# A second attention in phases of twelve tiles instead of eight, with its side steps placed ahead of each phase's last four tiles

## The chip, the cores and the metric

The kernel runs on one core of a Trainium2 chip. The metric is the device time of one execution in microseconds (us), lower is better. Before the change it is 3915.79 us, the median of three runs (3913.46 to 3922.16).

## What is computed

The program is one block of a hybrid model on x of 4 x 1024 tokens with 256 features, all in fp32: a causal attention, a mixture of experts, a second attention, and the mixture again, each added to its input. Only the second attention is changed. Cut to what matters:

```python
Xn = layernorm(X)                                  # x itself is a layernorm of the stage's input
P = einsum('btd,ed->bte', Xn, W_in) + b_in         # Q, K, V and a gate G, 16 heads of 16
sq = |Q|^2 + |K|^2 - 2 Q K^T                       # 1024 x 1024 per head, no causal mask
W = (1e-4 + sqrt(max(sq, 0))) ** -2
W = W / (1e-4 + sum(W))
out = X + einsum('btd,ed->bte', G * (W V), W_out) + b_out
```

## The kernel before

The stage is `attention_b`. A **unit** is one batch with one group of four heads (16 units); a **period** j is a unit with one half of its queries (512), 32 in all. In a period the keys are worked through in eight **tiles** m of 128 keys. So there are 256 tiles, g = 8 j + m. In the code b, p = divmod(j, 8): batch b, and period p of it. A tile passes through these steps, with `w` as its buffer of 128 x (4 heads x 512) values:

- `dist` on TensorE (L1958): squared distances of keys and queries, in two pairs of heads, each pair into one slot of a PSUM ring of **three slots**.
- `log` on ScalarE (L1869): logarithm of a pair from its slot into `w`; gives the slot back. It needs the table "natural_log" (loaded at L1919), and that the tile of `w` is free, which the values that last used it signal (`s_pv`).
- `bound` on VectorE (L1775): a lower bound for the logarithm.
- sigmoid on ScalarE (L1909), with the table "sigmoid_and_others" (loaded at L1906).
- squaring on VectorE (L1831): `w` times itself, the finished weight; signals `s_wts`.
- `values` on TensorE (L1946): weights times values, summed over a period's eight tiles in `acc`; it waits for `s_wts`.

Since logarithm and sigmoid are in different tables, ScalarE goes in blocks: eight sigmoids of a period, then eight logarithms of the next. VectorE makes eight squarings, then eight bounds.

Around that are **side steps**, in which TensorE takes one slot of the ring each:

- `tokens`: transposes the normalised tokens of a batch (L1971), copied out by ScalarE (L1877); `moments` (L1717) and `normalise` (L1732) on VectorE come before.
- `qkv` (n, x), L1982: projection for unit n, in two halves. VectorE's `take` (L1747 to L1755) reads the slot and gives it back. ScalarE squares Q and K (`squared`, L1893), VectorE sums them up (`lengths`, L1762).
- `stack` (n, i), L1992: transposes Q or K with their lengths; it waits until both `lengths` of the unit are done. VectorE's `operand` (L1769) copies it out and gives the slot back.
- `back` (j), L1999: transposes the finished sums of a period. It waits for `o_rows` (L1780, a copy of `acc` to `oT` on VectorE, which signals `s_oT`). `gates` (L1791 to L1796) on VectorE reads the slot, gives it back, and gates and normalises the result.
- `turn` and `project` (L1971, L2006, L2008), twice a batch: transpose the gated result (copied by ScalarE, `turned`, L1885) and project it, the bias by a matmul of its own. `add` (L1804) on VectorE gives the slot back.

TensorE works through one list, `ORDER`, in order. The other engines have their orders written out as loops; they and TensorE wait for each other by semaphores alone. An engine that waits in its list holds all that stands behind. A side step waits for its slot of the ring to be free, in the list's order of slots, as `dist` does: a slot comes round every third use.

In the order before, a plain period of TensorE is: values of tiles 0 to 2 with side steps between and behind them, the first distances of the next period, then values 3 and 4, and distances and values in turn, and the last four distances at the end:

```python
            if m == TB - 5:
                out += aux + ahead[:1]
            elif m > TB - 4:
                out += ahead[m - TB + 4:m - TB + 5]
            elif m < TB - 5:
                out += aux[:1]
```

`o_rows(j)` stands among the bounds after the period's squarings, and `gates(j)` ahead of the next period's squarings.

Of the kernel before, what the change touches and what calls it, by code (L numbers as in the profile page):

```python
# [22 lines left out]
P = 128  # L23
# [1483 lines left out]
def attention_b(nc, block, c, X, x, W, sem):  # L1507
# [11 lines left out]
    LAST = 2  # L1519
    SPAN = TB * P  # L1520

    def moved(j):

        out = [("back", j - 1, 0)] if 0 < j <= PERIODS else []
        b, p = divmod(j, TB)
        if j % 2 == 0 and j // 2 + 1 < UNITS:
            out += [("qkv", j // 2 + 1, x) for x in range(2)]
        if j % 2 and (j + 1) // 2 < UNITS:
            out += [("stack", (j + 1) // 2, i) for i in range(SIDES)]
        if p == 4 and b + 1 < B:  # L1530
            out += [("tokens", b + 1, x) for x in range(2)]
        if p < 2 and 0 < b < B or j > PERIODS:
            out += [("turn", b - 1, p), ("project", b - 1, p)]
        return out

    def first():

        out = [("tokens", 0, x) for x in range(2)] + [("qkv", 0, x) for x in range(2)]
        out += [("stack", 0, i) for i in range(SIDES)]
        return out + [("dist", 0, m) for m in range(TB)]  # L1540

    def order(j):

        ahead = [("dist", j + 1, m) for m in range(TB)] if j + 1 < PERIODS else []
        aux = moved(j)
        if j >= PERIODS:
            return aux
        if j == PERIODS - 1:
            last = [("values", j, m) for m in range(TB)]
            return aux + [("turn", B - 1, 0)] + last[:5] + [("project", B - 1, 0)] + last[5:]  # L1550
        out = aux[:2]
        aux = aux[2:]
        for m in range(TB):
            if m == TB - 5:
                out += aux + ahead[:1]
                aux = []
            elif m > TB - 4:
                out += ahead[m - TB + 4:m - TB + 5]
            elif m < TB - 5:
                out += aux[:1]  # L1560
                aux = aux[1:]
            out += [("values", j, m)]
        return out + ahead[4:]

    ORDER = [step for j in range(PERIODS + 2) for step in ((first() if j == 0 else []) + order(j))]
# [7 lines left out]
    with ExitStack() as ctx:  # L1573
# [5 lines left out]
        b_out = sb("b_out", [1, D])  # L1579
        row = sb("row", [1, P])  # L1580
# [10 lines left out]
        square = sb("square", [P, 2, TILES, HG, 2, DH])  # L1591
# [6 lines left out]
        w = sb("w", [P, TB, HG, QC])  # L1598
# [23 lines left out]
        s_last = sem("b_last_weights_ready")  # L1622
# [9 lines left out]
        def one(m):  # L1632
            return w[:, m].rearrange("p h n -> p (h n)")
# [18 lines left out]
        @block.sync  # L1652
        def _(sp):
            xv = x[0:B * L, :].rearrange("(t p) d -> p t d", p=P)
            for b in range(B):
                sp.dma_start(X[:, b * TB:(b + 1) * TB, :], xv[:, b * TB:(b + 1) * TB, :]).then_inc(s_x[b], 16)
                if b:
                    continue
                sp.dma_start(win[:], W["W_in"].rearrange("(c p) n -> p c n", p=P)).then_inc(s_w, 16)
                sp.dma_start(wo[:], W["W_out"].rearrange("(c p) n -> p c n", p=P)).then_inc(s_w, 16)  # L1660
                sp.dma_start(b_in[:], W["b_in"].partition_broadcast(P)).then_inc(s_w, 16)
                sp.dma_start(b_out[:], W["b_out"].unsqueeze(0)).then_inc(s_w, 16)

        WLOADS = 4 * 16
        INITS = 6

        @block.gpsimd
        def _(pool):
# [9 lines left out]
            def residual(b):  # L1678

                pool.drain()  # L1680
                pool.tensor_scalar(grow[:], rstd[:], 1.0, None, ALU.add)
                pool.tensor_tensor(drop[:], rstd[:], mv[:, :, 0], ALU.mult)
                pool.drain()
                pool.wait_ge(s_xn, b + 1)
                for t in range(TB):
                    pool.tensor_scalar(tile(b, t), tile(b, t), grow[:, t:t + 1], drop[:, t:t + 1], ALU.mult, ALU.subtract)
                pool.drain().then_inc(s_xadd, 1)
# [7 lines left out]
            pool.memset(row[:], 1.0).then_inc(s_init, 1)  # L1695
# [12 lines left out]
        def _(dve):  # L1708
# [26 lines left out]
            def take(n, x):  # L1735
# [14 lines left out]
                if n > 1:  # L1750
                    dve.wait_ge(s_pv, TB * 2 * (n - 1))
                    dve.wait_ge(s_gate, 2 * (n - 1))
# [19 lines left out]
            def bound(j, m):  # L1772

                R.wait_free(dve, AT["dist", j, m] + PAIRS - 1 + SLOTS, ())
                v.tensor_scalar(one(m), one(m), LOG_MIN, None, ALU.max).then_inc(s_bound, 1)  # L1775
# [45 lines left out]
            for m in range(TB):  # L1821
                bound(0, m)
            for j in range(PERIODS):
                b, p = divmod(j, TB)
                if j:
                    gates(j - 1)
                n = j // 2 + 1
                for m in range(TB):
                    if j < PERIODS - 1 or m < TB - LAST:
                        dve.wait_ge(s_sig, TB * j + m + 1)  # L1830
                        v.tensor_tensor(one(m), one(m), one(m), ALU.mult).then_inc(s_wts, 1)  # L1831
                    if n < UNITS:
                        if j % 2 == 0:
                            if m < 2:
                                take(n, m)
                            if m in (4, 5):
                                lengths(n, m - 4)
                        elif m < SIDES:
                            operand(n, m)
                    if b and p < 2 and m == 6:  # L1840
                        add(b - 1, p)
                    if j == PERIODS - 1 and m == TB - LAST:
                        add(B - 1, 0)
                for m in range(TB if j + 1 < PERIODS else 0):
                    bound(j + 1, m)
                    if m == 3:
                        o_rows(j)
                    if b + 1 < B and m == 3:
                        if p == 1:
                            moments(b + 1)  # L1850
                        if p == 3:
                            normalise(b + 1)
            o_rows(PERIODS - 1)
            gates(PERIODS - 1)
            add(B - 1, 1)
# [3 lines left out]
        def _(act):  # L1859
            s = nc.scalar  # L1860

            def log(j, m):

                at = AT["dist", j, m]
                if j:
                    act.wait_ge(s_pv, TB * (j - 1) + m + 1)
                for pair in range(PAIRS):
                    R.wait_ready(act, at + pair, ())
                    s.activation(w[:, m, 2 * pair:2 * pair + 2, :].rearrange("p h n -> p (h n)"), slot(at + pair), ACT.Ln,  # L1869
                                 scale=SHEP_EPS ** -2).then_inc(R.free[(at + pair) % SLOTS], 1)  # L1870
# [30 lines left out]
            for m in range(TB):  # L1901
                log(0, m)
            for j in range(PERIODS):
                b, p = divmod(j, TB)
                n = j // 2 + 1
                s.preload_act_table_set("sigmoid_and_others")  # L1906
                for m in range(TB):
                    act.wait_ge(s_bound, TB * j + m + 1)
                    s.activation(one(m), one(m), ACT.Sigmoid, scale=-0.5).then_inc(s_sig, 1)  # L1909
                    if j % 2 == 0 and n < UNITS and m in (3, 5):  # L1910
                        squared(n, (m - 3) // 2)
                    if p == 4 and b + 1 < B and m in (2, 4):
                        tokens(b + 1, m // 2 - 1)
                    if p < 2 and b and m == 4:
                        turned(b - 1, p)
                    if j == PERIODS - 1 and m == 2:
                        turned(B - 1, 0)
                if j + 1 < PERIODS:
                    s.preload_act_table_set("natural_log")  # L1919
                    for m in range(TB):  # L1920
                        log(j + 1, m)
            act.drain()
            for m in range(TB - LAST, TB):
                s.activation(one(m), one(m), ACT.Square).then_inc(s_last, 1)
            turned(B - 1, 1)

        @block.tensor
        def _(pe):
# [4 lines left out]
            for step in ORDER:  # L1933
                what, j, x = step
                n = AT[step]
                if what == "values":
# [4 lines left out]
                    if j < PERIODS - 1 or x < TB - LAST:  # L1941
                        pe.wait_ge(s_wts, TB * j + x + 1)
                    else:
                        pe.wait_ge(s_last, x - TB + LAST + 1)
                    for h in range(HG):
                        last = pe.matmul(acc[32 * h:32 * h + 32, qc, :], vg[:, u % 2, h, x, :], w[:, x, h, :],  # L1946
# [54 lines left out]
                elif what == "project":  # L2001
# [3 lines left out]
                    for t in range(TILES):  # L2005
                        pe.matmul(slot(n)[:, t * D:(t + 1) * D], row[:], b_out[:], start=True, stop=False)  # L2006
                        for cc in range(DC):
                            last = pe.matmul(slot(n)[:, t * D:(t + 1) * D], oTT[:, cc, t * P:(t + 1) * P], wo[:, cc, :],  # L2008
                                             start=False, stop=(cc == DC - 1))
# [82 lines left out]
```

## Time and profile before

| what | value |
|---|---|
| median of three runs | 3915.79 us |
| the profiled execution | 3922.57 us, its span 3920.8 us |
| second attention, first sigmoid table load to the end of the last add | 1796.87 to 2960.71 us of the span |
| TensorE busy over the span | 3543.4 us (90%) |
| VectorE busy over the span | 2494.0 us (64%) |
| ScalarE busy over the span | 2228.7 us (57%) |
| mean granted TensorE clock | 0.941 of full speed |

The span runs from the first to the last instruction; the execution's own time is 1.8 us longer. Busy shares are averages over four stages with different limits, so the stage of the change is read by itself below. In a row of instructions, a time in square brackets is the idle time of that engine just before it, and the name behind the arrow is what ended it. ACT is ScalarE, DVE VectorE, POOL GpSimd, PE TensorE's matmuls.

### The profile page before, as it was taken

What the parts mean: (1) busy time and instruction counts of PE and PEld (TensorE: products, weight loads), DVE (VectorE), ACT (ScalarE), POOL (GpSimd) and SP (SyncE); (2) the same over time, 40 slices, a digit from 0 to 9 for tenths busy, and PEclk for the clock granted to TensorE, in tenths of its full rate; (3) what the DMA queues carried; (4) which work ended last, traced back from release to release, by engine and by line L of the source; (5) the groups of instructions that cost most, each with busy time, mean ns of one, the idle gap of its engine ahead of it and who ended that gap; (6) DMA issues with size and microseconds to landing.
All of it is one profiled execution on the core that took longest, in us unless ns stands there. A gap on an engine that the chain in (4) does not pass through costs nothing.

```text
span 3920.8 us, 56053 instructions
## 1 busy us (share of the span) xinstructions
PE 3543.4 (90%) x22244; PEld 2491.0 (64%) x22244; DVE 2494.0 (64%) x4347; ACT 2228.7 (57%) x2875; POOL 646.5 (16%) x595
## 2 busy tenths in 40 slices
PE   4999999989999999978779779779877999999998
PEld 3555555478888899973323323323326888889998
DVE  4777777553433455547988988988985443335554
ACT  1666666643322344438998998998993332234443
POOL 3333332100122011221300300200000002200212
PEclk7999999899999999988889889889888999999999
DMA  3000000010011134430000000000001001013342
GB/s 123 1 1 1 1 1 1 1 65 6 25 37 32 34 94 115 105 76 8 1 1 1 1 1 1 1 1 1 1 1 65 6 22 38 24 45 91 94 111 40
DMA packets 86664, 124.81 MB, mean 32 GB/s; under 512 B 7752, under 2 KB 73115, under 8 KB 86402
## 3 DMA queue, kind: packets, MB, share of 16 engines
q1 hardware_dynamic: 68738, 100.05, 7.5%
q0 software_dynamic: 17664, 21.17, 3.3%
q8 instruction: 176, 2.88, 0.3%
q14 instruction: 86, 0.70, 0.1%
HBM read 85.02 MB, written 42.55 MB: 33 GB/s over the span
## 4 chain that ended last, share of the span: by engine, by line
PE 32%; ACT 10%; DVE 9%; issue 3%; DVEq 1%; ACTq 0%; POOL 0%; DMA 0%; SPq 0%; POOLq 0%
PE f2ring L1479 14%; PE f2acc L1498 7%; DVE b_w L1831 6%; ACT b_w L1869 5%; PE b_acc L1946 4%; PE b_ring L1958 4%; ACT b_w L1909 4%; ACT L1906 1%; PE b_ring L2008 1%; DVEq L1770 0%; PE b_ring L2006 0%; DVE b_stacks L1747 0%; PE b_ring L1982 0%; PE f2ring L1444 0%; DVE b_w L1775 0%
## 5 line engine op out<-in xcount | busy, mean ns | idle before, releaser
L1831 DVE TENSOR_TENSOR b_w<-b_w 128x2048 f32<-128x2048 f32 x254 | 571.7, 2292 | 25.7 <-ACT b_w L1909 21.7
L1869 ACT ACTIVATE b_w<-b_ring 128x1024 f32<-128x1024 f32 x512 | 485.9, 1037 | 92.2 <-PE b_ring L1958 86.3
L1946 PE MATMUL b_acc<-b_w,b_vg 128*32 128x512 f32 x2048 | 333.0, 740 | 172.6 <-DVE b_w L1831 171.5
L1909 ACT ACTIVATE b_w<-b_w 128x2048 f32<-128x2048 f32 x256 | 468.7, 1897 | 2.1 <-issue 0.4
L1399 ACT ACTIVATE f2hid<-f2ring 128x512 f32<-128x512 f32 (+2 forms) x256 | 132.6, 518 | 577.4 <-PE f2ring L1479 560.4
L1399 ACT ACTIVATE f1hid<-f1ring 128x512 f32<-128x512 f32 (+2 forms) x256 | 132.6, 518 | 576.8 <-PE f1ring L1479 559.8
L1317 DVE TENSOR_TENSOR f1hid<-f1hid,f1ring 128x512 f32<-128x512 f32 (+2 forms) x256 | 150.2, 587 | 439.4 <-ACT f1hid L1399 439.4
L1317 DVE TENSOR_TENSOR f2hid<-f2hid,f2ring 128x512 f32<-128x512 f32 (+2 forms) x256 | 150.2, 587 | 439.3 <-ACT f2hid L1399 439.2
L1958 PE MATMUL b_ring<-b_qT,b_kT 32*128 32x512 f32 x2048 | 411.4, 692 | 18.6 <-ACT b_w L1869 15.0
L1775 DVE TENSOR_SCALAR b_w<-b_w 128x2048 f32<-128x2048 f32 x256 | 305.7, 1225 | 86.7 <-ACT b_w L1869 85.8
L624 ACT ACTIVATE a_prob<-a_wide 128x1024 f32<-128x1024 f32 (+1 forms) x320 | 292.8, 943 | 86.5 <-PE a_wide L730 59.6
L1479 PE MATMUL f1ring<-f1xh,f1wg 128*128 128x512 f32 (+2 forms) x1536 | 326.1, 354 | 10.5 <-DVE f1xh L1300 8.2
L1479 PE MATMUL f2ring<-f2xh,f2wg 128*128 128x512 f32 (+2 forms) x1536 | 326.1, 354 | 10.0 <-DVE f2xh L1300 7.7
L1958 PEld LDWEIGHTS b_ring<-b_qT,b_kT 32*128 32x128 f32 x2048 | 129.3, 197 | 307.3 <-issue 152.1
L1946 PEld LDWEIGHTS b_acc<-b_w,b_vg 128*32 128x32 f32 x2048 | 48.3, 121 | 402.6 <-DVE b_w L1831 296.1
L522 DVE CUSTOM_DVE_ANT_0 a_deep<-a_deep,a_edge 128x128 f32<-128x128 f32 (+3 forms) x512 | 241.8, 516 | 90.8 <-PE a_deep L700 85.8
L1479 PEld LDWEIGHTS f1ring<-f1xh,f1wg 128*128 128x128 f32 x1536 | 250.6, 190 | 35.4 <-DVE f1xh L1300 9.1
L1479 PEld LDWEIGHTS f2ring<-f2xh,f2wg 128*128 128x128 f32 x1536 | 250.7, 190 | 35.0 <-DVE f2xh L1300 8.6
L1498 PEld LDWEIGHTS f1acc<-f1wd,f1hh 128*128 128x128 f32 x1536 | 200.7, 191 | 17.3 <-DVE f1hh L1145 7.9
L1498 PEld LDWEIGHTS f2acc<-f2wd,f2hh 128*128 128x128 f32 x1536 | 200.7, 191 | 17.3 <-DVE f2hh L1145 7.8
L1498 PE MATMUL f1acc<-f1wd,f1hh 128*128 128x256 f32 x1536 | 204.7, 283 | 5.8 <-DVE f1hh L1145 5.8
L1498 PE MATMUL f2acc<-f2wd,f2hh 128*128 128x256 f32 x1536 | 204.7, 283 | 5.7 <-DVE f2hh L1145 5.7
(340 smaller groups left out, 6274.9 us busy)
## 6 DMA issues: line engine op xcount, KB each, us to landing
X<-expert_in SPq DMA_DIRECT2D x16, 650.0 KB, 4.8
expert_in<-a_zeros SPq DMA_DIRECT2D x8, 650.0 KB, 10.1
X<-in_x SPq DMA_DIRECT2D x4, 1024.0 KB, 10.7
x_mid<-X SPq DMA_DIRECT2D x8, 512.0 KB, 3.1
f1raw_x<-in_rd SPq DMA_DIRECT2D x4, 1024.0 KB, 5.3
f1raw_xf<-in_rg SPq DMA_DIRECT2D x4, 1024.0 KB, 5.0
f1raw_xf<-in_ru SPq DMA_DIRECT2D x4, 1024.0 KB, 7.1
f1raw_g<-in_rg SPq DMA_DIRECT2D x4, 1024.0 KB, 4.9
```

The source lines that it names most:

```text
L522: v.tensor_tensor_reduce(got, got, edge[:, CHUNK - n:], 1.0, LOWEST, ALU.add, ALU.max, peak).then_inc(s_dve, 1)
L624: s.activation(dst, src.rearrange("p (h e n) -> p h e n", h=2, e=pairs)[:, :, :, 0:n], ACT.Exp).then_inc(s_act, 1)
L1317: v.tensor_tensor(hid[:, s % 2, 0:n], hid[:, s % 2, 0:n], slot(step)[:, QC:QC + n], ALU.mult).then_inc(free_of(step), 1)
L1399: s_eng.activation(hid[:, s % 2, 0:n], slot(step)[:, 0:n], ACT.Silu).then_inc(s_silu, 1)
L1479: last = pe.matmul(dst[:, j * QC:j * QC + n], w[:, a, cc, i * P:(i + 1) * P], xh[:, b, x, cc, first:first + n], start=(k == 0 and cc == 0) ...
L1498: last = pe.matmul(acc[:, g % 2, t * D:(t + 1) * D], hh[:, s % 2, a, t * P:(t + 1) * P], w[:, part, i, :], start=(i == 0 and k == 0 and t ...
L1775: v.tensor_scalar(one(m), one(m), LOG_MIN, None, ALU.max).then_inc(s_bound, 1)
L1831: v.tensor_tensor(one(m), one(m), one(m), ALU.mult).then_inc(s_wts, 1)
L1869: s.activation(w[:, m, 2 * pair:2 * pair + 2, :].rearrange("p h n -> p (h n)"), slot(at + pair), ACT.Ln, scale=SHEP_EPS ** -2).then_inc(R. ...
L1909: s.activation(one(m), one(m), ACT.Sigmoid, scale=-0.5).then_inc(s_sig, 1)
L1946: last = pe.matmul(acc[32 * h:32 * h + 32, qc, :], vg[:, u % 2, h, x, :], w[:, x, h, :], start=(x == 0), stop=(x == TB - 1))
L1958: last = pe.matmul(slot(n + e)[:, h * QC:(h + 1) * QC], kT[at, u % 2, x * P:(x + 1) * P], qT[at, u % 2, qc * QC:(qc + 1) * QC], start=True ...
```

## The change

The tiles are no longer grouped by period but in runs ("phases") of twelve: 21 of twelve tiles and one of four. `w` holds twelve tiles. ScalarE makes twelve sigmoids, then the logarithms of the twelve tiles after; VectorE twelve squarings, then twelve bounds. A tile g's distances are made for the tile twelve further on. In TensorE's list a phase has first the side steps and values of its first eight tiles, then the side steps of its last four tiles, then two tiles of distances, and then values and distances in turn. The side steps have places by m (`beside`): qkv at 1 and 2 and stacks at 6 and 7 of even periods, back at 2, turn at 5 and project at 7, tokens at 5 and 6. VectorE's side work moves too: `o_rows` of the period before behind squaring m=1, `gates` behind m=3, `take` behind m=2 and 3, `lengths` behind 5 and 6, `operand` behind 6 and 7, all inside the loop of squarings. ScalarE's `squared` stands behind sigmoids 4 and 5, its token copies behind 6 and 7.

Beside that: the output bias is no longer added by matmuls on TensorE but by GpSimd to X (`residual`), for which it is loaded to all partitions; `square` shares memory with the upper half of `xn`; the last two tiles are squared on VectorE like all others, where ScalarE did it.

```diff
+    RUN = 12
+    ALL = TB * PERIODS
+    RUNS = [range(g, min(g + RUN, ALL)) for g in range(0, ALL, RUN)]
+    def beside(j, m):
+
         b, p = divmod(j, TB)
+        n = j // 2 + 1
+        out = []
+        if j % 2 == 0 and n < UNITS:
+            if m in (1, 2):
+                out += [("qkv", n, m - 1)]
+            if m in (6, 7):
+                out += [("stack", n, m - 6)]
+        if p == 5 and b + 1 < B and m in (5, 6):
+            out += [("tokens", b + 1, m - 5)]
+        if m == 2 and j:
+            out += [("back", j - 1, 0)]
+        if p < 2 and b:
+            if m == 5:
+                out += [("turn", b - 1, p)]
+            if m == 7:
+                out += [("project", b - 1, p)]
         return out
...
+        for run in RUNS:
+            ahead = [d for g in run for d in dist(g + RUN)]
+            late = run[len(run) - 4:]
+            for g in run:
+                out += beside(*divmod(g, TB))
+                if g not in late:
+                    out += [("values", *divmod(g, TB))]
+            out += ahead[:2]
+            ahead = ahead[2:]
+            for g in late:
+                out += [("values", *divmod(g, TB))] + ahead[:1]
+                ahead = ahead[1:]
+            out += ahead
...
         ...

+            for run in RUNS:
+                for g in run:
+                    dve.wait_ge(s_sig, g + 1)
+                    v.tensor_tensor(one(g), one(g), one(g), ALU.mult).then_inc(s_wts, 1)
+                    if j % 2 == 0 and n < UNITS:
+                        if m in (5, 6):
+                            lengths(n, m - 5)
+                        if m in (6, 7):
+                            operand(n, m - 6)
+                    if j and m == 1:
+                        o_rows(j - 1)
+                    if j and m == 3:
+                        gates(j - 1)
+                    if j % 2 == 0 and n < UNITS and m in (2, 3):
+                        take(n, m - 2)
+                    if b and p < 2 and m == 7:
                         add(b - 1, p)
+                    if p == 5 and b + 1 < B and m == 2:
+                        normalise(b + 1)
+                for g in run:
+                    if g + RUN < ALL:
+                        bound(g + RUN)
...

+                pool.drain()
+                pool.tensor_tensor(xs, xs, b_out[:].unsqueeze(1).to_broadcast([P, TB, D]), ALU.add)
```

## Rows read from the trace of the kernel before

**Rows 1.** The page's first line.
```profile
span 3920.8 us, 56053 instructions
```

**Rows 2.** Timeline: the stage's first sigmoid table load and its last instruction.
```profile
1796.87 1.28 ACT L1906 ACT_TABLE_LOAD   x1
...
2959.49 1.22 DVE L1804 TENSOR_TENSOR X<-X,b_ring 128x1024 f32<-128x1024 f32 x1 [13.08 <-PE b_ring L2008]
```

**Rows 3.** Windows, the stage's steady part: its length, then each engine's busy time.
```profile
1797.00:2935.00 1138.00, 930.03 (x5097) 341.41 (x5097) 1028.54 (x922) 1044.87 (x864) 88.36 (x36) 0.87 0.00 1
```

**Rows 4.** Groups of instructions in the stage: busy us, mean ns, idle before.
```profile
L1869 ACT ACTIVATE b_w<-b_ring 128x1024 f32<-128x1024 f32 x512 | 485.9, 1037 | 92.2 <-PE b_ring L1958 86.3
L1906 ACT ACT_TABLE_LOAD x32 | 41.1, 1283 | 0.6
L1919 ACT ACT_TABLE_LOAD x31 | 39.8, 1283 | 0.5
```

**Rows 5.** Timeline of a plain odd period, ScalarE and VectorE.
```profile
2270.73 1.28 ACT L1906 ACT_TABLE_LOAD   x1
...
2272.02 14.51 ACT L1909 ACTIVATE b_w<-b_w 128x2048 f32<-128x2048 f32 x8
...
2273.97 2.29 DVE L1831 TENSOR_TENSOR b_w<-b_w 128x2048 f32<-128x2048 f32 x1 [0.74 <-ACT b_w L1909]
2276.18 1.22 DVE L1769 COPY b_qT<-b_ring 128x1024 f32<-128x1024 f32 x1
...
2277.53 2.29 DVE L1831 TENSOR_TENSOR b_w<-b_w 128x2048 f32<-128x2048 f32 x1
...
2281.09 13.30 DVE L1831 TENSOR_TENSOR b_w<-b_w 128x2048 f32<-128x2048 f32 x6
...
2305.02 1.28 ACT L1906 ACT_TABLE_LOAD   x1
```

**Rows 6.** Timeline: an operand's wait for its stack, and a take.
```profile
1776.67 1.22 DVE L1769 COPY b_qT<-b_ring 128x1024 f32<-128x1024 f32 x1 [1.19 <-PE b_ring L1992]
...
2310.46 0.75 DVE L1747 TENSOR_TENSOR b_stacks<-b_ring,b_b_in 128x256 f32<-128x256 f32 x2
...
2311.79 2.28 DVE L1831 TENSOR_TENSOR b_w<-b_w 128x2048 f32<-128x2048 f32 x1
```

**Rows 7.** Timeline at the stage's end: oT copy, back and gates.
```profile
2943.61 0.69 DVE L1780 COPY b_oT<-b_acc 128x512 f32<-128x512 f32 x1 [1.45 <-PE b_acc L1946]
2944.36 0.42 PEld L1999 LDWEIGHTS b_ring<-ident,b_oT 128*128 128x128 f32 x4 [1.72 <-DVE b_oT L1780]
...
2945.05 0.17 DVE L1791 TENSOR_SCALAR b_den<-b_ring 128x16 f32<-128x16 f32 x1 [0.75 <-PE b_ring L1999]
...
2945.98 0.42 DVE L1796 TENSOR_TENSOR b_gated<-b_gate,b_den 128x256 f32<-128x256 f32 x1
```

**Rows 8.** Timeline of the last full period: distances and logarithms in turn.
```profile
2902.45 3.77 ACT L1869 ACTIVATE b_w<-b_ring 128x1024 f32<-128x1024 f32 x4
...
2903.53 1.13 PE L1958 MATMUL b_ring<-b_qT,b_kT 32*128 32x512 f32 x4 [1.68 <-ACT b_w L1869]
...
2905.58 1.14 PE L1958 MATMUL b_ring<-b_qT,b_kT 32*128 32x512 f32 x8
...
2906.81 4.00 ACT L1869 ACTIVATE b_w<-b_ring 128x1024 f32<-128x1024 f32 x4 [0.59 <-PE b_ring L1958]
...
2911.18 7.44 ACT L1869 ACTIVATE b_w<-b_ring 128x1024 f32<-128x1024 f32 x8 [0.36 <-PE b_ring L1958]
```

**Rows 9.** Timeline of TensorE after a longer wait, period 4.
```profile
1959.21 2.08 PE L1958 MATMUL b_ring<-b_qT,b_kT 32*128 32x512 f32 x4 [3.67 <-ACT b_w L1869]
...
1965.85 1.38 PE L1958 MATMUL b_ring<-b_qT,b_kT 32*128 32x512 f32 x8
```

**Rows 10.** Timeline of GpSimd: a batch's scalings beside a busy VectorE.
```profile
1932.86 24.39 POOL L1686 TENSOR_SCALAR X<-X,b_grow,b_drop 128x256 f32<-128x256 f32 x8 [63.55 <-DVE b_xn L1732]
```

**Rows 11.** Timeline of ScalarE: first logarithms at a batch's start.
```profile
2105.59 1.94 ACT L1869 ACTIVATE b_w<-b_ring 128x1024 f32<-128x1024 f32 x2 [6.39 <-PE b_ring L1958]
```

## Prediction on record

> **What bounds the kernel now.** I read the cores' view first, then the stage's windows, its groups of instructions, the stage's timeline and the chain of waits. The profiled execution took 3922.57 us, of which 3920.8 us are the span [rows 1]; it stands 6.8 us above the median of 3915.79. Only the second attention changes. From its first table load for the sigmoids to its last add it takes 1796.87 to 2959.49 + 1.22 = 2960.71, that is 1163.8 us [rows 2]. In its steady part VectorE is busy 1028.5 and ScalarE 1044.9 of 1138 us [rows 3]: both are nearly full, so any time that one of them waits for TensorE is paid. ScalarE alternates a block of sigmoids and a block of logarithms with a table load ahead of each, 32 of the first kind and 31 of the second at 1283 ns [rows 4].
>
> The reader is to see in [rows 5] how one period of eight tiles goes. ScalarE makes a sigmoid each (14.51 - 1.90) / 7 = 1.80 us. VectorE starts its first squaring 3.24 us after the table load, and then needs (13.30 - 2.29) / 5 = 2.20 us a tile, so it falls behind ScalarE by 0.4 us a tile and by its side work on top. The values of a tile wait for this squaring, and the distances that stand behind values in TensorE's order wait with it. Logarithms need distances. Who is late at the phase's end is therefore VectorE, then TensorE, then ScalarE.
>
> **What is removed.** 256 tiles in phases of twelve are 22 phases: 22 and 21 table loads for 32 and 31, so 20 x 1.283 = 25.7 us less on ScalarE. The Trainium skill (ScalarE: Activation LUTs, What ACT_TABLE_LOAD costs) puts a switch at about 2.66 us, a drain included; by that estimate it would be 53 us less. The trace disagrees: the sigmoids start 1.29 us after the load's start [rows 5]. I take 25.7, and it is contained in the timetable below. The bias matmuls of eight projects also go; they lie beside other work, but for the last project.
>
> **What the new order does.** This I found by putting the positions in the two lists side by side, not in a row: TensorE takes all side steps of a phase's last four tiles *before* the two distances ahead and before those four values. But these steps wait for VectorE work that VectorE does *after* squarings of these same last four tiles: back waits for the copy of the sums behind the squaring of tile m=1, both stacks wait for the second lengths behind m=6. TensorE is in order, so the distances and ScalarE's logarithms are held. On top, the three slots of the ring pass through the side steps, and a slot is given back by take (m=2, 3), gates (m=3) or operand (m=6, 7), again behind late squarings.
>
> **Durations for the timetable** (from a phase's first table load; VectorE's squaring i ends at 5.44 + 2.20 i plus side work): one take 2311.79 - 2310.46 = 1.33, operand 2277.53 - 2276.18 = 1.35, wait from lengths to the first operand 1.2 [rows 5, 6]; oT copy to start of back 0.75, gates about 1.35 [rows 7]; lengths 0.6 (estimated a little under the oT copy's 0.69). TensorE's tail I take from the last full period [rows 8]: with W the moment it may go on with the second half of distance 1, W is 2903.53, distance 2 starts at 2905.58 = W+2.05 behind one tile of values, its logarithm at 2906.81 = W+3.28, the one two tiles on at 2911.18, 4.37 later, the next after some 2.1; then TensorE is ahead and a logarithm tile takes 2 x (7.44 - 1.02) / 7 = 1.83. From the fifth distance's logarithm at W+9.75 seven tiles remain: the phase ends at W+22.7.
>
> That is at the full clock. After TensorE idled 3.67 us the same chain began at half speed: the half distance took 2.08 us where the fast one took 1.13, and the second distance after it started at 1965.85, W+6.64 [rows 9], where the fast one has 2.05 and a pitch of 2.1. That is 2.5 more: W+25.2 in the slow case. By the end of it the clock is back. The new order makes TensorE idle more than that before W in three of four phases, so the slow case is the nearer row. The Trainium skill (TensorE: Matmul & The Clock Gate, Why this matters for your kernels) warns of such gaps between bursts of matmuls; by that rule, the trace agrees, the sum would be the slow one below.
>
> **Four kinds of phases**, by where the last four tiles lie (fast / slow):
> - A, m=0..3 of an odd period (6 phases). Side work ahead of squaring 9: two takes, oT, gates, two lengths, the wait and two operands, 9.8 us; squaring 9 ends at 35.0, oT 35.7, back, distance 0 at 36.6. Distance 1 needs back's slot, which gates gives back behind squaring 11 (40.1), at 40.7 = W. 63.4 / 65.9.
> - B, m=4..7 of an even period (5). TensorE is held at the stacks until lengths behind squaring 10 (33.5); distance 1 needs the second stack's slot, given back by the operand behind squaring 11: W = 39.4, or 39.9 with slow stacks. 62.1 / 65.1.
> - C, m=0..3 of an even period (5). Two qkv and back fill the ring. The slots come back at the take behind squaring 10 (31.5), and behind squaring 11, gates and take at 36.4. W = 37.2 to 37.4. 60.1 / 62.5.
> - D, m=4..7 of an odd period (5). No side steps last. Distance 0 follows the values of the eighth tile at 27.7; the following values wait for squarings, which end at 30.2, 32.4, 34.6 and 36.8; the fifth distance's logarithm starts at 39.4, and seven tiles follow. 52.4 either way.
>
> Each is the time of twelve tiles, for which 1.5 plain periods of 34.3 [rows 5] took 51.5.
>
> Corrections: A: first phase -2.0 (nothing to take back), one with normalise +2.7, one with project and add +3.7, and the 21st phase, which has only four distances ahead and no takes, is 40.3 / 42.8. B: a late project +2.8, a project in front with add +5.4. C: moments +1.9, project and add +5.5, normalise +2.7. D: normalise, then both token transposes ahead of the distances with a sigmoid behind their copy, +8.5; late turn and project, whose slot the add gives back, +10.8. Each is worked out in the same way, by where the moved step holds VectorE or a slot. Sums: A 361.7 / 376.7, B 318.7 / 333.7, C 310.6 / 322.6, D 281.3 / 283.8. The last phase of four tiles with back, turns and projects, takes 38 (an estimate: four squarings, then back, gates, and two turns and projects one behind the other). Four more tiles of distances before the first load: 4 x 1.83 = 7.3. Total 1317.6 / 1362.1 for 1163.8: **+154 / +198 us**.
>
> **Costed at nothing.** GpSimd's added bias sum runs where no one waits: I bound it by the same engine's eight scalings, 24.4 us beside VectorE [rows 10]; X is next needed by moments or add some 100 us later. If it slowed VectorE as the scalings do, it would be under 1 us a batch; if its batch came late, add would hold VectorE for up to 24 us, three times, 73 at the upper end. I take nothing: its cover is over twice its length. The square buffer that now shares xn, and the wider b_out load, stand where no wait is near; 0 to 1 us.
>
> The squared steps now wait on ScalarE for take (1.0 and 2.5 us in A), but ScalarE has its sigmoids and load done at 29 there, and the distances come at 38.
>
> I take three quarters of the way from fast to slow, since A, B and C idle long before W: +187, against 3915.79 that is **4103 us**.
>
> **Rivals.**
> 1. *Side steps are hidden, phases bound by squarings only.* Then every phase goes like D: 20 x 53 + 39 + 38 + 7 + some 15 at the batches = 1159, no change: 3911. For it: before, side steps stood between values without a hold. Against: the waits above are in the code. Chance 0.04.
> 2. *Faster:* distances ahead are ready whenever ScalarE has loaded its table, 24 to 29 us into a phase, and 20 phases take VectorE's own 48.5 + 0.7: 984 + 39 + 38 + 7 + 18 = 1086, so 3838. Table loads saved and the batch boundaries (6.39 us of idle ScalarE at one of them [rows 11]) speak for it. It decides at the start of distance 0: before 29 us it holds, after that it does not. Chance 0.03.
> 3. *TensorE at half clock through the whole tail.* Four pitches of 4.0 instead of 2.1 in 19 phases: some +145 over the fast case, near 4215. Against: in [rows 9] the clock came back after some 5 us. Chance 0.05.
> 4. *Part of the hold only* (say one of the slot waits missing or the takes earlier), +50 to +125: 3965 to 4040. Chance 0.08.
> 5. The forecast: 0.80.
>
> **Range.** Fast and slow sums give 4070 and 4114; an error of 1.5 us a phase over 20 phases is 30 more on each side: 4040 to 4144, rounded to 4040 to 4150. It leaves out rivals 1 to 4 (0.20). A measurement of this kernel can tell about 0.2% from no change; faster by more 0.04, within 0.02, slower 0.94.
>
> **What would show it.** In the profile after: 22 and 21 table loads; ScalarE's idle before its logarithms, 92 us here [rows 4], at 250 or more, released by TensorE's distances; long idle of TensorE released by the oT copy (back) and by lengths (stacks), and of distances by gates and operands; table load to table load 61 to 66 us in three phases of four and about 53 in the fourth. If TensorE reaches distance 0 before ScalarE's second load in kinds A to C, the prediction is wrong.

## The result, and the profile after

The changed kernel takes 4140.1 us (median, 4138.1 to 4147.1) against 3916.5 us beside it: ratio 1.0572, 95% interval 1.0554 to 1.0591. The forecast was 4103 us, range 4040 to 4150. The kernel is 224 us slower where 187 were forecast.

The page of the changed kernel, its span and three groups of its stage (busy us, mean ns, idle before). The first answers to [rows 4].

```profile
span 4139.7 us, 55907 instructions
...
L1881 ACT ACTIVATE b_w<-b_ring 128x1024 f32<-128x1024 f32 x512 | 482.1, 1068 | 251.2 <-PE b_ring L1965 247.0
L1845 DVE TENSOR_TENSOR b_w<-b_w 128x2048 f32<-128x2048 f32 x256 | 576.6, 2288 | 54.3 <-ACT b_w L1922 50.9
L1953 PE MATMUL b_acc<-b_w,b_vg 128*32 128x512 f32 x2048 | 350.4, 769 | 256.1 <-DVE b_w L1845 256.1
```

The logarithms themselves did not get dearer: 482.1 us busy for 485.9 in [rows 4]. A squaring takes 2288 ns, about the 2.29 us of [rows 5]. ScalarE's idle time before its logarithms is 251 us where it was 92, and TensorE's distances end it. The third row is TensorE's values: they wait 256.1 us for squarings. The 20 table loads are saved as counted:

```profile
L1916 ACT ACT_TABLE_LOAD x22 | 28.2, 1283 | 0.4
L1930 ACT ACT_TABLE_LOAD x21 | 26.9, 1283 | 0.5
```

The waits view of the stage after (who waited for whom, us in total, times, longest) shows both directions:

```profile
ACT b_w L1881 <- PE b_ring L1965: 247.0, 87, 11.3
ACT b_xn L1905 <- DVE b_stacks L1759: 72.7, 22, 3.9
PE b_ring L1999 <- DVE b_stacks L1774: 58.2, 15, 8.7
ACT b_xnT L1889 <- PE b_ring L1978: 40.1, 5, 16.1
ACT b_xn L1897 <- PE b_ring L1978: 31.6, 7, 7.0
PE b_ring L2006 <- DVE b_oT L1796: 31.3, 7, 5.4
DVE b_qT L1781 <- PE b_ring L1999: 29.9, 16, 2.1
PE b_ring L1965 <- DVE b_gate L1767: 22.8, 7, 7.0
DVE b_stacks L1759 <- PE b_ring L1989: 16.3, 8, 2.7
DVE b_den L1807 <- PE b_ring L2006: 13.9, 10, 1.5
```

TensorE waits for VectorE at the stacks (L1999), at back (L2006) and for slots that take gives back (L1767): the hold that was forecast. VectorE waits for TensorE at the stacks' copy (L1781), at take (L1759) and at gates (L1807): of this the forecast had only the wait at the stacks, at 1.2 us a unit, and the other two at nothing. ScalarE's account of the stage has 159 us more idle before logarithms, 66 more at `squared` (6.3 before), 43 more at token and turn copies (28.9 before), and 26 less for table loads, in sum 242. The stage from its first statistics to its last add takes 1206.8 us before and 1434.7 after, 228 more. The 14 us between are ScalarE's too: 7.0 less behind its last copy, 3.7 for the two squares that it no longer makes, 3.8 less in logarithms. The whole span grows by 219 us and not 228, since the stages ahead of this one ended 9.2 us sooner in the profile after.

The fifth phase, one of kind A, in the timeline after (start, us, engine, idle before):

```profile
2060.18 1.28 ACT L1916 ACT_TABLE_LOAD   x1
...
2073.11 0.76 DVE L1759 TENSOR_TENSOR b_stacks<-b_ring,b_b_in 128x256 f32<-128x256 f32 x2 [2.40 <-PE b_ring L1989]
...
2078.19 0.17 DVE L1807 TENSOR_SCALAR b_den<-b_ring 128x16 f32<-128x16 f32 x1 [1.47 <-PE b_ring L2006]
...
2090.72 1.22 DVE L1781 COPY b_qT<-b_ring 128x1024 f32<-128x1024 f32 x1 [2.06 <-PE b_ring L1999]
...
2095.84 4.49 DVE L1845 TENSOR_TENSOR b_w<-b_w 128x2048 f32<-128x2048 f32 x2
2100.25 0.69 DVE L1796 COPY b_oT<-b_acc 128x512 f32<-128x512 f32 x1
...
2100.99 1.12 PE L2006 MATMUL b_ring<-ident,b_oT 128*128 128x128 f32 x4 [5.27 <-DVE b_oT L1796]
2102.04 2.09 PE L1965 MATMUL b_ring<-b_qT,b_kT 32*128 32x512 f32 x8
2104.22 1.94 ACT L1881 ACTIVATE b_w<-b_ring 128x1024 f32<-128x1024 f32 x2 [11.26 <-PE b_ring L1965]
...
2105.81 2.09 PE L1965 MATMUL b_ring<-b_qT,b_kT 32*128 32x512 f32 x8 [1.68 <-DVE b_gate L1808]
...
2131.39 1.28 ACT L1916 ACT_TABLE_LOAD   x1
```

Read it from the end. TensorE may go on with distance 1 at 2105.81, when gates gives back's slot: that is W, 45.6 us into the phase, forecast 40.7. From W to the next table load are 25.6 us, forecast 25.2. Before that TensorE idled 5.27 us for the copy of the sums, and ScalarE 11.26 us. Of the 4.9 us by which W is late, 4.7 are VectorE's three waits above: 2.40 at take, 1.47 at gates, and 2.06 at the stack's copy where 1.2 was counted.

The phases, from one sigmoid table load to the next, in us, by kind (the forecast, fast / slow, is for the sum of the kind):

| kind | after | sum | forecast |
|---|---|---|---|
| A (phases 1, 5, 9, 13, 17, 21) | 67.7, 71.2, 72.7, 69.7, 70.0, 41.5 | 392.8 | 361.7 / 376.7 |
| B (2, 6, 10, 14, 18) | 65.8, 67.0, 72.2, 64.6, 69.2 | 338.8 | 318.7 / 333.7 |
| C (3, 7, 11, 15, 19) | 65.9, 67.0, 62.9, 73.3, 62.9 | 332.0 | 310.6 / 322.6 |
| D (4, 8, 12, 16, 20) | 66.0, 53.9, 65.4, 54.2, 54.0 | 293.5 | 281.3 / 283.8 |
| last, to the last add | 27.5 | 27.5 | 38 |

### The profile page after: what moved, and what is told of

The parts are those of the page before. It is cut to its first block, busy times and chain, and to the rows that moved or that the text cites. A ratio compares the mean times of both kernels' runs of the same rounds, so it can differ in the third digit from the quotient of the medians.

```text
span 4139.7 us, 55907 instructions
## 1 busy us (share of the span) xinstructions
PE 3573.7 (86%) x22180; PEld 2505.7 (61%) x22180; DVE 2521.1 (61%) x4349; ACT 2196.5 (53%) x2853; POOL 658.5 (16%) x598
## 4 chain that ended last, share of the span: by engine, by line
PE 32%; DVE 13%; ACT 9%; issue 2%; DVEq 1%; POOL 0%; DMA 0%; ACTq 0%; SPq 0%; POOLq 0%
PE f2ring L1479 13%; DVE b_w L1845 9%; PE f2acc L1498 7%; ACT b_w L1881 6%; PE b_ring L1965 4%; PE b_acc L1953 4%; PE b_ring L1989 2%; ACT b_w L1922 2%; PE b_ring L1999 1%; DVEq L1809 1%; ACT L1916 1%; PE b_ring L2014 1%; PE b_ring L1978 0%; DVE b_stacks L1774 0%; DVE b_oT L1796 0%
## 5 line engine op out<-in xcount | busy, mean ns | idle before, releaser
L1881 ACT ACTIVATE b_w<-b_ring 128x1024 f32<-128x1024 f32 x512 | 482.1, 1068 | 251.2 <-PE b_ring L1965 247.0
L1845 DVE TENSOR_TENSOR b_w<-b_w 128x2048 f32<-128x2048 f32 x256 | 576.6, 2288 | 54.3 <-ACT b_w L1922 50.9
L1953 PE MATMUL b_acc<-b_w,b_vg 128*32 128x512 f32 x2048 | 350.4, 769 | 256.1 <-DVE b_w L1845 256.1
L1965 PE MATMUL b_ring<-b_qT,b_kT 32*128 32x512 f32 x2048 | 437.8, 702 | 52.8 <-DVE b_gate L1767 22.8
L1787 DVE TENSOR_SCALAR b_w<-b_w 128x2048 f32<-128x2048 f32 x256 | 320.2, 1261 | 208.4 <-ACT b_w L1881 207.9
L1965 PEld LDWEIGHTS b_ring<-b_qT,b_kT 32*128 32x128 f32 x2048 | 138.4, 200 | 339.3 <-ACT b_w L1881 169.7
## 6 DMA issues: line engine op xcount, KB each, us to landing
X<-in_x SPq DMA_DIRECT2D x4, 1024.0 KB, 10.7
```

The costliest lines, as they stand in the source:

```text
L1787: v.tensor_scalar(one(g), one(g), LOG_MIN, None, ALU.max).then_inc(s_bound, 1)
L1845: v.tensor_tensor(one(g), one(g), one(g), ALU.mult).then_inc(s_wts, 1)
L1881: s.activation(w[:, g % RUN, 2 * pair:2 * pair + 2, :].rearrange("p h n -> p (h n)"), slot(at + pair), ACT.Ln, scale=SHEP_EPS ** -2).then_ ...
L1965: last = pe.matmul(slot(n + e)[:, h * QC:(h + 1) * QC], kT[at, u % 2, x * P:(x + 1) * P], qT[at, u % 2, qc * QC:(qc + 1) * QC], start=True ...
```

## Experiments

### Undo the hold alone

```diff
             for g in run:
-                out += beside(*divmod(g, TB))
+                for step in beside(*divmod(g, TB)):
+                    if g not in late or step[0] in ("tokens", "turn"):
+                        out += [step]
...
             for g in late:
+                out += [step for step in beside(*divmod(g, TB)) if step[0] not in ("tokens", "turn")]
                 out += [("values", *divmod(g, TB))] + ahead[:1]
```

> The changed kernel, but in the last four tiles of a phase each side step stands just ahead of the values of its own tile, behind the two distances that are ahead (tokens and turn stay in front, since ScalarE copies them between its sigmoids). Theory A (TensorE is held at side steps whose sources and slots VectorE gives only behind late squarings): distance 0 follows the values of a phase's eighth tile, so the phases with side steps last (kinds A, B, C, 62 to 73 us) fall to 54 to 60, the kind without them (54) stays; in all 20 x 57 + 41 + 27 + 7 = 1215 us for the stage against 1392 after and 1171 before counted alike, so about 3960 us (3920 to 4010). Theory B (a phase of twelve makes VectorE lag, and that is what costs): all phases stay above 60 and the time above 4080. Theory C (half clock of TensorE): the time falls by less than 60 us, since the clock stays low.

Measured: 4062.8 us, ratio to before 1.0376 (1.0358 to 1.0393), 77 us less than the changed kernel. Theory A is right in what moves and what doesn't: kind A's phases sum to 338.9 (54 less), B's to 321.2 (18 less), C's to 315.4 (17 less), D's to 293.0 for 293.5. Its number, 3960, was missed by 103 us: plain phases of A to C stop at 59 to 62 us, not 54 to 60, and those with tokens or turns stay at 63 to 71. Theory B's 4080 or more and theory C's fall of less than 60 us are both missed too. The mean granted clock rose from 0.922 to 0.935 with the edit, and how much of the 77 us came by way of the clock was not separated. So the hold at late side steps is shown, and it is a third of the loss. The timeline of the fifth phase here:

```profile
2046.94 1.28 ACT L1919 ACT_TABLE_LOAD   x1
...
2060.36 0.76 DVE L1762 TENSOR_TENSOR b_stacks<-b_ring,b_b_in 128x256 f32<-128x256 f32 x2 [2.88 <-PE b_ring L1992]
...
2065.44 0.17 DVE L1810 TENSOR_SCALAR b_den<-b_ring 128x16 f32<-128x16 f32 x1 [1.47 <-PE b_ring L2009]
...
2077.97 1.23 DVE L1784 COPY b_qT<-b_ring 128x1024 f32<-128x1024 f32 x1 [2.06 <-PE b_ring L2002]
...
2079.33 2.29 DVE L1848 TENSOR_TENSOR b_w<-b_w 128x2048 f32<-128x2048 f32 x1
...
2081.68 1.06 PE L1956 MATMUL b_acc<-b_w,b_vg 128*32 128x512 f32 x8 [1.05 <-DVE b_w L1848]
2082.68 1.99 PE L1968 MATMUL b_ring<-b_qT,b_kT 32*128 32x512 f32 x12
...
2083.91 3.77 ACT L1884 ACTIVATE b_w<-b_ring 128x1024 f32<-128x1024 f32 x4 [3.69 <-PE b_ring L1968]
2084.99 1.13 PE L1968 MATMUL b_ring<-b_qT,b_kT 32*128 32x512 f32 x4 [0.33 <-ACT b_w L1884]
...
2108.58 1.28 ACT L1919 ACT_TABLE_LOAD   x1
```

ScalarE now waits 3.69 us for distance 0 instead of 11.26, and TensorE makes half a distance in 1.13 us, as at the full clock in [rows 8]. But distance 0 starts only 35.7 us into the phase, where kind D was forecast at 27.7: it follows the values of the eighth tile, and the squaring of that tile ends at 34.7. VectorE's three waits are still there, 2.88, 1.47 and 2.06 us, all ahead of this squaring: 6.4 us that the expected 54 to 60 held only in part. In how far they explain it was not tested in this run.

### The phase's length

```diff
-    RUN = 12
+    RUN = 8
```

> The changed kernel with phases of eight tiles instead of twelve, so a phase is a period, and the last four tiles are always m = 4 to 7. The placing of side steps stays. Theory A: in even periods both stacks stand before distance 0 and wait for the second lengths behind squaring 6, and the operand behind squaring 7 gives the slot for distance 1: W = 30.4 and the period ends at about 46 to 48; odd periods hold nothing and take about 34.5; so 16 pairs of 81 for 68.8: +190 us, 4080 to 4130 us. Theory B (the longer phase costs): near the kernel before, 3900 to 3960 us.

Measured: 4198.1 us in a single run, outside 4080 to 4130, in the direction that theory A gives and further. Even periods take 50 to 54 us, plain odd ones 37. With the side steps placed as they are, a short phase does not mend the kernel, so the length is not what costs. The same pair without the hold:

> The run sides_with_their_tiles with phases of eight instead of twelve, so that the two runs differ in the phase's length alone and neither takes side steps of late tiles ahead of the distances. Theory A2 (what is left of the loss after undoing the hold is VectorE's and TensorE's waiting for each other inside the squarings, which a phase of eight with the same places shares): 3990 to 4070 us, near the 4063 of twelve tiles. Theory B (a phase of twelve is what is left): 3900 to 3950 us.

Measured: 4126.2 us, one run, above both ranges, that of theory A2 too. Plain even periods take 47, odd ones 35 to 37, so 82 to 84 for 16 tiles, where twelve-tile phases with the same places take 59 to 62 (54 for one in four) for 12. At the same places of side steps, phases of twelve are 58 us (first pair) and 63 us (second pair) *faster* than phases of eight. Theory B is out in both pairs. The last run has the phase length of the kernel before and is still 209 us slower than it: so much lies in the new places of side steps and distances and the small parts beside them. What phases of twelve are worth with the places of the kernel before was not run.

### VectorE's side of the waiting

```diff
-            if m in (1, 2):
-                out += [("qkv", n, m - 1)]
+            if m in (0, 1):
+                out += [("qkv", n, m)]
```

> The changed kernel with qkv in TensorE's list at m=0 and 1 instead of 1 and 2, so the two takes of VectorE and back, which stands behind the second, find TensorE done. In the trace after, a phase of kind A (first tiles m=0 to 7 of an even period) waits 2.4 us at a take and 1.5 us at gates inside the squarings. If these waits are what the forecast missed in kind A (71 us for 66), its phases fall by 3 to 4 us each and kind B by 1 to 3, the others stay: 4105 to 4125 us. If the miss is TensorE's clock, the phases fall by less than 1 us: 4135 us or more.

Measured: 4110.5 us, one run, within 4105 to 4125; the profiled span is 31 us shorter than that of the changed kernel. Kind A: 64.1, 65.7, 68.3, 66.4, 66.8, that is 3.6, 5.5, 4.4, 3.3 and 3.2 less; B 8 less in sum, C 1 and D 1. In the fifth phase the first take no longer waits. The first `squared` waits 0.82 us; the first row below is the changed kernel's, the other two are this run's:

```profile
2073.89 0.63 ACT L1905 ACTIVATE b_xn<-b_stacks 128x512 f32<-128x512 f32 x1 [3.31 <-DVE b_stacks L1759]
...
2060.71 0.75 DVE L1759 TENSOR_TENSOR b_stacks<-b_ring,b_b_in 128x256 f32<-128x256 f32 x2
...
2061.49 0.63 ACT L1905 ACTIVATE b_xn<-b_stacks 128x512 f32<-128x512 f32 x1 [0.82 <-DVE b_stacks L1759]
```

This is the part that the forecast missed in kind A. The other way round, VectorE's gates closer behind back:

```diff
-                    if j and m == 1:
+                    if j and m == 0:
                         o_rows(j - 1)
-                    if j and m == 3:
+                    if j and m == 2:
                         gates(j - 1)
```

> The changed kernel with the copy of the sums moved from behind squaring m=1 to behind m=0, and gates from behind m=3 to behind m=2. TensorE's list is untouched. Theory A: in kind A (last tiles m=0 to 3 of an odd period) distance 0 comes one squaring earlier and the slot for distance 1 too, so its six phases are 2.2 us shorter each, the others shorter or longer by under 1.5 us: 4120 to 4135 us, with the wait of distances for gates ending one squaring sooner in those phases. Theory C (what costs is TensorE's clock or the number of distances ahead): no phase changes by more than 0.5 us.

Measured: 4188.8 us, one run, 49 us slower, where theory A had 5 to 20 us less and theory C no change. It is a miss: phases 1, 5, 9 and 15 fell, by 1.2 to 1.6 us and not 2.2, and the others rose, by up to 6.3. Two lines of its waits and the timeline of its fifth phase say why:

```profile
ACT b_xn L1905 <- DVE b_stacks L1759: 107.2, 22, 10.9
...
DVE b_den L1807 <- PE b_ring L2006: 74.8, 25, 7.8
```

```profile
2088.68 0.17 DVE L1807 TENSOR_SCALAR b_den<-b_ring 128x16 f32<-128x16 f32 x1 [7.80 <-PE b_ring L2006]
```

Gates now comes before TensorE has got through two qkv and back, so VectorE stands in the middle of its squarings, 74.8 us in all instead of 13.9. Nothing that TensorE issues changed. The same queue of VectorE carries the squarings, and each wait in it delays them all.

### Distances further ahead

```diff
-            out += ahead[:2]
-            ahead = ahead[2:]
-            for g in late:
+            out += ahead[:3]
+            ahead = ahead[3:]
+            for i, g in enumerate(late):
...
-                out += [("values", *divmod(g, TB))] + ahead[:1]
-                ahead = ahead[1:]
+                out += [("values", *divmod(g, TB))] + ahead[:TAKE[i]]      # TAKE = (2, 2, 1, 1)
+                ahead = ahead[TAKE[i]:]
```

> The run sides_with_their_tiles (4063 us), but with three tiles of distances ahead of the late values, and then 2, 2, 1, 1 distances behind each of the four values instead of one each. Left of the loss there are 54 us in each phase without late side steps for 51.5 before, because the late values, which follow VectorE's squarings, stand between the distances. Theory A (distances held behind late values are the next cost): such a phase falls by 2 to 3 us to 51 to 52, and the others too: 4000 to 4020 us. Rival (VectorE's own chain, its waits for qkv and stacks, sets these phases): within 10 us of 4063, and the waits of VectorE for TensorE stay or grow.

Measured (the edit stands on sides_with_their_tiles): 4089.5 us, ratio 1.0437 (1.0422 to 1.0452), 27 us *slower* than the run it is built on. Distances held behind late values are not the next cost. By the waits view, distances wait 56.6 us for logarithms to free their slots where they waited 44.9, the side steps of the late tiles stand behind the third distance, and VectorE waits for those:

```profile
DVE b_qT L1786 <- PE b_ring L2004: 85.4, 16, 13.9
DVE b_stacks L1764 <- PE b_ring L1994: 63.6, 14, 12.9
DVE b_den L1812 <- PE b_ring L2011: 61.3, 21, 4.9
```

These three are 55.3, 38.7 and 27.3 us in sides_with_their_tiles. With qkv earlier as well, where its period does not begin in the last four tiles:

> Both edits together on sides_with_their_tiles: side steps with their tiles, three distances ahead, and qkv one tile earlier wherever its period does not begin in the last four tiles. If the costs are separate (holds, distances behind late values, takes waiting for qkv), they add: 10 to 20 us less than three_distances_ahead, 3985 to 4010 us. If VectorE's chain is the bound already, about the same as three_distances_ahead. In neither case below the 3917 us of the kernel before, since VectorE still waits at the stacks and its squarings lag by a phase of twelve.

Measured: 4058.3 us, ratio 1.0357 (1.0342 to 1.0372): 31 us less than the run before it, more than the 10 to 20 expected, but from a higher start, so that the expected 3985 to 4010 was missed. And without the third distance:

> sides_with_their_tiles (4063 us) with qkv at m=0 and 1 wherever its period doesn't begin in the last four tiles. The same step gave 3 to 5 us in each phase of kind A when the late side steps stayed in front, 31 us in all. If the two costs are separate, it gives 25 to 31 us here too: 4030 to 4040 us; if the hold's removal had hidden these waits, 4055 or more. Either way slower than the kernel before.

Measured: 4037.3 us, ratio 1.0311 (1.0295 to 1.0326), within 4030 to 4040. Undoing the hold (77 us) and moving qkv (26 us on top of it, 30 alone) add up nearly: these are separate costs. With qkv moved too, the third distance costs 21 us.

### The bias on GpSimd

> The changed kernel without GpSimd's sum of the output bias to X; the output bias is missing from the result, nothing else. In the trace after, one gates instruction on VectorE took 3.81 us instead of 0.43 while that sum ran on GpSimd. If the two share a path, this phase (the fifteenth, 73.3 us) is 3 to 5 us shorter and the other 21 stay: 4130 to 4138 us. If that instruction waited for something else, the phase stays at 73.3.

The edit takes the sum out of `residual`, so that the result lacks the output bias. Measured: 4142.4 us, one run, above the expected 4130 to 4138; the total can't tell. The fifteenth phase fell from 73.3 to 69.9, within the expected 3 to 5 and the largest move of any. The others were to stay: those ahead of it moved by up to 1.5 either way, those behind it by 0.1 at most. The two timelines of this phase, first of the changed kernel, then of this one:

```profile
2764.11 6.64 POOL L1699 TENSOR_TENSOR X<-X,b_b_out 128x2048 f32<-128x2048 f32 x1
...
2767.23 3.81 DVE L1812 TENSOR_TENSOR b_gated<-b_gate,b_den 128x256 f32<-128x256 f32 x1
...
2772.42 3.78 PE L1965 MATMUL b_ring<-b_qT,b_kT 32*128 32x512 f32 x12 [7.04 <-DVE b_gate L1767]
```

```profile
2771.51 0.43 DVE L1810 TENSOR_TENSOR b_gated<-b_gate,b_den 128x256 f32<-128x256 f32 x1
...
2773.32 3.79 PE L1963 MATMUL b_ring<-b_qT,b_kT 32*128 32x512 f32 x12 [3.66 <-DVE b_gate L1765]
```

The kernel before with this part of the change alone (row and the bias matmuls out, GpSimd's sum in, as in the diff above):

> The kernel before with one part of the change alone: the output bias summed by GpSimd instead of by matmuls on TensorE. Before, the first logarithms of a batch's first period start 6.4 us late and 2.1 us late in its second, behind a projection of 6.8 to 10 us, of which the bias matmuls are 2.5 to 4. If that is on the path, 3 batches x (3 + 1.5) and some 5 us at the stage's end are gained, less up to 4 us a batch where GpSimd's sum holds a VectorE instruction: 3895 to 3910 us, ratio 0.995 to 0.998. If these matmuls were hidden, no change, 3917 us.

Measured: 3906.9 us, ratio 0.9971 (0.9961 to 0.9980): faster, within the expected times, but not where expected. In the two profiles the whole gain of the stage is at its end: from the last sigmoid table load to the last add 34.8 us for 42.1. Another 4 us of the profiled difference lie ahead of the stage's first sigmoid table load, and were not taken apart. The last add's wait for its projection, 13.08 us in [rows 2], is

```profile
2948.14 1.22 DVE L1805 TENSOR_TENSOR X<-X,b_ring 128x1024 f32<-128x1024 f32 x1 [8.84 <-PE b_ring L2008]
```

The batches give nothing: the first period of a batch takes 40.5 for 42.5, but the second 40.4 for 37.8. This is the one version here that beats the kernel before. A second part on top of it (the tokens' transposes in a batch's sixth period, `p == 5` for `p == 4` in TensorE's and ScalarE's order):

> before_with_bias_on_gpsimd (0.9971 of before) with a second part of the change: the transposes of a batch's normalised tokens in the sixth period of a batch (two stacks beside them) instead of the fifth (two qkv beside them). Before, the fifth period takes 41.0 us for 34.5 of a plain even one, with 1.6 us of wait for a token copy and 3.0 us for distances. If the crowd of side steps makes this, the sixth takes some 37 for 34.2 and the fifth 34.5: 3 x 3.7 = 11 us, 3893 to 3900 us, ratio 0.993 to 0.996. If the tokens cost the same wherever they stand, 3905 us.

Measured: 3918.9 us, ratio 1.0007 (0.9998 to 1.0016), a miss: the gain of the bias is gone. The fifth period of a batch falls to 35.3 from 40.1 to 42.1, but the sixth rises to 43.5 to 44.2 from 34. Why tokens cost more beside stacks than beside qkv was not taken apart.

## Why the prediction came out as it did

- *TensorE is held at side steps of the last four tiles.* Right, and shown by undoing it: kinds A, B and C shrink, D stays. Its size is another matter: undoing it was expected to bring 177 us and brought 77. The rest of the lengthening stays without the hold. The forecast's total is near, and in that there is some luck.
- *W and the tail behind it.* Right in form. Tail 25.6 for 25.2, at the slow clock, as taken. Plain C 62.9 for 62.5, plain B 64.6 for 65.1, plain D 54 for 52.4.
- *The term that was mis-sized is the side work inside the squarings of kind A*, counted as 9.8 us of VectorE time ahead of squaring 9. In the fifth phase it is 14.9: that squaring ends 40.1 us into the phase, forecast 35.0. VectorE waits for qkv, back and the stack, which TensorE issues one behind the other, partly at half clock (the first qkv takes 5.35 us at a mean granted clock of 0.69, the second 3.72 at 1.00). The forecast asked what TensorE waits for and took for granted that VectorE's takes and gates find their slots full. Kind A is 16 us over the slow sum; moving qkv one tile up gave back 20.
- *Tokens and turns.* Too low: phases 4, 10, 12 and 15 are 5, 7, 2 and 8 us over what the corrections gave. In phases 10 and 15 the tokens lie among the first eight tiles, and the forecast has no term for them there. ScalarE's copies stand between sigmoids, and those of tokens wait 12.0, 2.7 and 8.7 us for TensorE in phases 4, 10 and 15; the squarings wait for the sigmoids behind them. In phase 15 another 3.4 us are GpSimd's sum, which was costed at nothing. That split rests on the profile, and the 3.4 on a single run beside it.
- *The last phase* was too high by 10.5 us, since the projects run at the full clock without the bias matmuls, in 3.72 us each, where the last one took 10.7 before.
- *Rival 1* (no change) and *rival 2* (faster) fall with the first logarithms of kind A, 44.0 us into the phase, where 29 would decide. *Rival 3* (half clock through the whole tail) falls with the tail of 25.6. *Rival 4* (a part of the hold only) falls with the phases of 63 to 73 us.
- The forecast errors add up to 30 us over the slow sum, and the forecast stood 11 below that sum. The measured median is 37 above the forecast and within the range.

Open: of the 120 us that sides_with_tiles_and_qkv_earlier is still above the kernel before, the waits of VectorE inside its squarings are named by the profile, but no run here took them all away. Nor did any run put VectorE's side work back where the kernel before has it, so what its place inside the squarings costs by itself is not shown.

## What to carry to other kernels

When a step is moved ahead in one in-order queue, write beside it where its source is made and where its buffer is given back in the other queues, counted in the same steps: a step put ahead of the work that its source stands behind holds all that follows. Do the same from the consumer's side, for every wait that the move puts into the middle of another engine's main loop. A change with several parts is to be measured in parts: here the longer phase gained 58 and 63 us at the new places of side steps, the bias sum 11 us on the kernel before, and the places of side steps hid both.

## What the runs showed of the hardware

A VectorE instruction stood while a long GpSimd instruction ran. In the changed kernel the last product of gates took 3.81 us instead of 0.43 and ended 0.29 us after GpSimd's sum of 2048 elements a partition. The Trainium skill (GPSIMD Engine Reference, Specifications) has the two share their SBUF interfaces, with contention for VectorE instructions with two SBUF inputs or in a two-port mode; the trace agrees. In before_with_bias_on_gpsimd it is the bounds, which have one tensor input, four of which take 4.63 us elsewhere:

```profile
1953.28 9.29 POOL L1688 TENSOR_TENSOR X<-X,b_b_out 128x2048 f32<-128x2048 f32 x1
...
1956.96 9.16 DVE L1776 TENSOR_SCALAR b_w<-b_w 128x2048 f32<-128x2048 f32 x4
```

It is so for two more of the four sums of the changed kernel: three bounds beside each took 7.80 and 7.68 us, where one takes 1.23, and these two sums took 4.56 and 4.53 us. It is not every such instruction: within the 6.64 us of the last sum, a squaring before the gates product kept its 2.28 us and a product with an input in PSUM its 0.42, and the sum itself was 2.1 us longer than the 4.51 that the first sum takes, beside which VectorE was idle or copying from PSUM. So one of the two seems to stand while the other runs. Which one goes first was not taken apart: in the next batch of before_with_bias_on_gpsimd the sum (9.28 us) began 0.7 us behind two squarings; these and a bound right behind them kept their times, and two bounds after a gap of 0.27 us took 6.33 us instead of 2.36.
